# Rounding on ScalarE and two-deep loads in the weight quantisation of a transformer layer

## The chip, the cores and the metric

The program runs on all 8 cores of one Trainium2 chip, each with its own share of the batch and with a full copy of the weights to prepare. Time is device microseconds from the first to the last instruction of the slowest core; lower is better. The engines are TensorE (PE in the profile), VectorE (DVE), ScalarE (ACT), GpSimd (POOL) and SyncE (SP). SP and POOL also issue DMA transfers; each core has 16 DMA engines, shared by both queues.

## The reference

One layer, 16 sequences of 2048 x 1024 float32: attention with 16 heads, then a feed-forward block whose weights are quantised to -1, 0 and 1, each with layer norms and a residual.

```python
def weight_quant(w):
    scale = 1.0 / jnp.clip(jnp.mean(jnp.abs(w)), 1e-05)
    return jnp.clip(jnp.round(w * scale), -1, 1) / scale
def bit_linear(x, w):        # act_quant: 8 bits for each row of x
    return einsum('bsd,hd->bsh', act_quant(x), weight_quant(w))
x = x + layernorm(attn(layernorm(x)))
h = silu(depthwise_conv1d(bit_linear(layernorm(x), w1)))   # w1: 4096 x 1024
x = x + layernorm(bit_linear(h, w2))                       # w2: 1024 x 4096
```

## The kernel before

Each core takes two sequences and all weights. Its work is cut into stages by an all-engine barrier of the core: the setup (weights), then per sequence layer norm, the q, k and v products, attention, the output product, and last the two feed-forward products. No core waits for another.

The setup writes prepared weights to DRAM, from where later stages load them. It first casts wq, wk, wv and wo to bf16 (eight batches of 2 MB; stores of wqkv_sp at L235). Then `quant_weight` runs for w1 and after it for w2, each 16 MB in float32, in `nbatch` = 8 batches of 2 MB: a tile `stg[sl]` (named wstg in the profile) of 128 x 4096. For w1 one batch is one block of 128 rows of 16 KB, for w2 four blocks of 4 KB rows. There are two such tiles, sl = c % 2, two output tiles `wqx` (wqa, wqb), and a single `qh16` in float16.

`quant_weight` has two passes. The absmean pass loads all batches and sums absolute values on DVE (L264 the load, L269 the sum), followed by a short chain that puts the scale into `wsc` (L273 to L293). The quantising pass loads all batches again (L311), and DVE does three operations for each: L316 multiplies by the scale, adds 1536 and rounds to an integer by writing float16 (qh16); L320 subtracts 1536 and takes the maximum with -1; L323 takes the minimum with 1. Then the batch is stored as bf16, 1 MB (L326).

In this pass even batches are loaded by SP, odd ones by POOL, and all stores are issued by POOL. Each engine's instructions run in program order, and the load of batch c stands in iteration c: behind a wait for the clamp (L323) of batch c-2, and on POOL behind the store of batch c-1, which waits for the clamp of that batch. `Sem.wait(engine, value)` makes an engine wait; without a value it waits for all that was issued so far. After w2 SP waits for all transfers, and the barrier at L334 ends the setup. `posRM` is a 128 x 1 tile that holds 1536. ScalarE is not used in the setup.

Of the kernel before, what the change touches and what calls it, by code (L numbers as in the profile page):

```python
# [12 lines left out]
AF = mybir.ActivationFunctionType  # L13
AX = mybir.AxisListType
OP = mybir.AluOpType
# [7 lines left out]
RM = 1536.0  # L23
# [16 lines left out]
def build_nc(dbg=()):  # L40
# [3 lines left out]
    def _un(n):  # L44
        _nctr[0] += 1
        return f"{n}_{_nctr[0]}"
# [27 lines left out]
    V, S, TE, G, SY = nc.vector, nc.scalar, nc.tensor, nc.gpsimd, nc.sync  # L74
# [8 lines left out]
    with es:  # L83
# [14 lines left out]
        posRM = sbuf("posRM", [128, 1], F32)  # L98
        wsc = sbuf("wsc", [128, 4], F32)
# [21 lines left out]
        sv, ss, st, sg = (sems[k] for k in ["tv", "ts", "tt", "tg"])  # L121
        dxr = [sems["dxr0"], sems["dxr1"], sems["dxr2"], sems["dxr3"]]
        dstg = [sems["dst0"], sems["dst1"]]
        dss = [sems["dss0"], sems["dss1"]]
# [54 lines left out]
        qh16 = _ph.enter_context(nc.sbuf_tensor(_un("qh16"), [128, DH], F16))  # L179
# [3 lines left out]
        with _ph:  # L183
            stg = [wstg0, wstg1]
# [34 lines left out]
            for i, (wh, b) in enumerate([(w, k) for w in range(3) for k in range(2)]):  # L219
                eng = SY if i % 2 == 0 else G  # L220
                if i >= 2:
                    sv.wait(eng, castv[i - 2])
                lv = dstg[i % 2].inc(eng.dma_start(
                    stg[i % 2][:, 0:4 * H].rearrange("p (c n) -> p c n", n=H),
                    wsrc[wh][b * 512:(b + 1) * 512, :].rearrange(
                        "(c p) n -> p c n", p=128)), 16)
# [13 lines left out]
            for b in range(2):  # L240
                sl = b % 2
                eng = SY if sl == 0 else G
                sv.wait(eng, castv[-2])
                lv = dstg[sl].inc(eng.dma_start(
                    stg[sl][:, 0:4 * H].rearrange("p (c n) -> p c n", n=H),
                    wo_h[b * 512:(b + 1) * 512, :].rearrange(
                        "(c p) n -> p c n", p=128)), 16)
# [4 lines left out]
            def quant_weight(src_h, nchunk, width, sw_col, dst_sp, mwcol=None):  # L252
                nb = DH // width
                nbatch = nchunk // nb
                bw = nb * width
                redv = []
                sv.wait(SY)
                sv.wait(G)
                for c in range(nbatch):
                    if c >= 2:  # L260
                        sv.wait(SY, redv[c - 2])
                        sv.wait(G, redv[c - 2])
                    eng = SY if c % 2 == 0 else G
                    lv = dstg[c % 2].inc(eng.dma_start(  # L264
                        stg[c % 2][:, 0:bw].rearrange("p (c n) -> p c n", n=width),
                        src_h[c * nb * 128:(c + 1) * nb * 128, :].rearrange(
                            "(c p) n -> p c n", p=128)), 16)
                    dstg[c % 2].wait(V, lv)
                    redv.append(sv.inc(V.tensor_reduce(  # L269
                        nrm[:, c % 16:c % 16 + 1], stg[c % 2][:, 0:bw],  # L270
                        axis=AX.X, op=OP.add, apply_absolute_value=True)))
                sv.wait(V)
                sv.inc(V.tensor_reduce(nrm[:, 20:21], nrm[:, 0:nbatch],  # L273
                                       axis=AX.X, op=OP.add))
                sv.wait(TE)
                tq1 = st.inc(TE.matmul(pst[0:1, 0:128], nrm[:, 20:21], identf[:],  # L276
                                       start=True, stop=True))
                st.wait(V, tq1)
                sv.inc(V.tensor_reduce(nrm[0:1, 21:22], pst[0:1, 0:128],
                                       axis=AX.X, op=OP.add))  # L280
                sv.wait(TE)
                tq2 = st.inc(TE.matmul(pst[:, 0:1], ones1f[:], nrm[0:1, 21:22],
                                       start=True, stop=True))
                st.wait(V, tq2)
                sv.inc(V.tensor_copy(nrm[:, 21:22], pst[:, 0:1]))
                sv.wait(V)
                sv.inc(V.reciprocal(nrm[:, 22:23], nrm[:, 21:22]))
                sv.wait(V)
                nel = float(nchunk * 128 * width)
                sv.inc(V.tensor_scalar(wsc[:, sw_col:sw_col + 1], nrm[:, 22:23], nel,  # L290
                                       None, op0=OP.mult))
                if mwcol is not None:
                    sv.inc(V.tensor_scalar(wsc[:, mwcol:mwcol + 1], nrm[:, 21:22],  # L293
                                           1.0 / (nel * 127.0), None, op0=OP.mult))
                sv.wait(V)
                qv = [0, 0]
                qst = [0, 0]
                sv.wait(SY)
                sv.wait(G)
                dss[0].wait(V)  # L300
                dss[1].wait(V)
                dsq[0].wait(V)
                dsq[1].wait(V)
                for c in range(nbatch):
                    sl = c % 2
                    if c >= 2:
                        sv.wait(SY, qv[sl])
                        sv.wait(G, qv[sl])
                        dss[sl].wait(V, qst[sl])
                    eng = SY if c % 2 == 0 else G  # L310
                    lv = dstg[sl].inc(eng.dma_start(  # L311
                        stg[sl][:, 0:bw].rearrange("p (c n) -> p c n", n=width),
                        src_h[c * nb * 128:(c + 1) * nb * 128, :].rearrange(
                            "(c p) n -> p c n", p=128)), 16)
                    dstg[sl].wait(V, lv)
                    sv.inc(V.tensor_scalar(qh16[:, 0:bw], stg[sl][:, 0:bw],  # L316
                                           wsc[:, sw_col:sw_col + 1], RM,
                                           op0=OP.mult, op1=OP.add))
                    sv.wait(V)
                    sv.inc(V.tensor_scalar(wqx[sl][:, 0:bw], qh16[:, 0:bw],  # L320
                                           -RM, -1.0, op0=OP.add, op1=OP.max))
                    sv.wait(V)
                    qv[sl] = sv.inc(V.tensor_scalar(wqx[sl][:, 0:bw], wqx[sl][:, 0:bw],  # L323
                                                    1.0, None, op0=OP.min))
                    sv.wait(G, qv[sl])
                    qst[sl] = dss[sl].inc(G.dma_start(  # L326
                        dst_sp[c * nb:(c + 1) * nb].rearrange("c p n -> p c n"),
                        wqx[sl][:, 0:bw].rearrange("p (c n) -> p c n", n=width)), 16)

            quant_weight(w1t_h, KC, DH, 0, w1qt_sp, mwcol=1)  # L330
            quant_weight(w2t_h, HC, H, 2, w2qt_sp)
            for s_ in (dstg[0], dstg[1], dss[0], dss[1], dsq[0], dsq[1], dc):
                s_.wait(SY)
# [4 lines left out]
        with _ph:  # L338
            A3 = attA[:, :].rearrange("p (c n) -> p c n", n=T)

            for s in range(NSEQ):
# [7 lines left out]
                with _ph:  # L349
# [6 lines left out]
                    for i in range(NT128):  # L356
# [3 lines left out]
                        if i >= 2:  # L360
                            st.wait(S, lnuse[i % 2])
                        sev = ss.inc(S.activation(ln1b[i % 2][:], xr[i % 3][:], AF.Identity,  # L362
                                                  scale=r_ap, bias=mb_ap))
# [39 lines left out]
                with _ph:  # L403
# [36 lines left out]
                    for oc in range(OC):  # L440
# [5 lines left out]
                        if oc + 1 < OC:  # L446
                            sl2 = (oc + 1) % 2
                            eng = SY if sl2 == 0 else G
# [4 lines left out]
                        for j in range(NT512):  # L453
# [18 lines left out]
                            for kc in range(KC):  # L472
# [10 lines left out]
                                                      bias=bq_pre[:, oc:oc + 1]))  # L483
# [5 lines left out]
                                                      scale=1.0, bias=bv_pre[:, oc:oc + 1]))  # L489
# [95 lines left out]
                with _ph:  # L585
# [80 lines left out]
                    for g in range(NPAIR * NSTEP):  # L666
                        p, i = divmod(g, NSTEP)
                        qc, kt = divmod(i, NKT)
                        sl = g % 2
                        if pend[0] is not None and i in (2, 10, 18, 26):  # L670
                            flush_tailA((2, 10, 18, 26).index(i))
                        if i == 2 * NKT + 4 and pend[0] is not None:
# [7 lines left out]
                            bias=negM[:, p:p + 1], scale=1.0))  # L680
# [53 lines left out]
                with _ph:  # L734
# [11 lines left out]
                    for g in range(8):  # L746
# [34 lines left out]
                        for i in range(2):  # L781
# [7 lines left out]
                                                      scale=r3, bias=mb3))  # L789
# [17 lines left out]
                        for i in range(2):  # L807
# [8 lines left out]
                                                      scale=r2, bias=mb2))  # L816
# [8 lines left out]
                                                   None, op0=OP.max))  # L825
# [14 lines left out]
                                                   op0=OP.mult, op1=OP.add))  # L840
# [3 lines left out]
                                op0=OP.add))  # L844
# [59 lines left out]
        with _ph:  # L904
# [18 lines left out]
            for s in range(NSEQ):  # L923
# [81 lines left out]
                for ti in range(NT128):  # L1005
# [14 lines left out]
                                           op0=OP.max))  # L1020
# [4 lines left out]
                                           None, op0=OP.mult))  # L1025
# [40 lines left out]
        with _ph:  # L1066
# [79 lines left out]
            for idx in range(NSJ):  # L1146
# [6 lines left out]
                for i2 in range(2):  # L1153
                    for half in range(2):
# [4 lines left out]
                            for c in range(HC):  # L1159
                                base = c * 512 + (i2 * 2 + half) * 128  # L1160
                                for hh in range(2):
# [13 lines left out]
                                                      scale=r4, bias=mb4))  # L1175
# [49 lines left out]
```

How the kernel before makes its waits and increments, by code:

```python
    def inc(self, ins, n=1):  # L31
        ins.then_inc(self.h, n)
        self.v += n
        return self.v
# [1 line left out]
    def wait(self, eng, v=None):  # L36
        eng.wait_ge(self.h, self.v if v is None else v)
```

## Time and profile before

| | us |
|---|---|
| median of the runs shown (2 runs) | 4776.24 |
| lowest and highest of them | 4764.93, 4787.56 |
| the profiled execution | 4804.53 |
| its span, slowest core (core 0) | 4802.9 |
| spans of the other cores | 4744.0 to 4796.4 |

The profile shows one execution. Its page gives for each engine the busy share in 40 equal slices of the span (one slice is 120 us). In the timeline a line is one instruction: start, duration, engine, source line, operation, output and input tiles, and in brackets how long the engine had been idle and what ended that. SPq and POOL lines with DMA_DIRECT2D are the issue of a transfer, not the transfer itself. In the table of windows each line gives, for a stretch of time, the busy time of each engine with its number of instructions, then TensorE's granted clock (1.00 is full), the mean busy share of the 16 DMA engines and what they moved in GB/s.

### The profile page before, as it was taken

To read this page: it belongs to the slowest core of one execution; us is meant where nothing else is said; L and a number is where in the kernel's file an instruction comes from. 1 tells how busy PE (TensorE), PEld (TensorE's weight loads), DVE (VectorE), ACT (ScalarE), POOL (GpSimd) and SP (SyncE) were. 2 spreads that over 40 slices of the span, in tenths; PEclk is the share of its full clock that TensorE was granted. 3 is DMA by queue.
4 is the path that set the end of the run, shared out by engine and by line. 5 is a ranking of instruction groups with operands and counts; after the bars stand their busy time and mean duration, and the time that the engine had idled before them with its cause. 6 is when DMAs were issued, how large, how long until landed. Compare 5 with 4: busy or idle time off the path is not lost. (4 is left out here: it accounts for less than half of the span.)

```text
span 4802.9 us, 42027 instructions; the slowest of 8 cores (4744.0 to 4802.9 us)
## 1 busy us (share of the span) xinstructions
PE 2892.2 (60%) x12214; PEld 1071.8 (22%) x12366; DVE 2091.1 (44%) x3552; ACT 1786.7 (37%) x2139; POOL 67.6 (1%) x110
## 2 busy tenths in 40 slices
PE   0000177888884231687888852329985986476877
PEld 0000033222221111332222211113332332132333
DVE  1443434446464444343555554434443444334332
ACT  0000133878782212337787832112221221424231
POOL 0001000000000000000000000000000000000000
PEclk9999999999996665899999976559997997687888
DMA  7675200000000222100000002231111111432231
GB/s 202 239 233 196 95 33 20 1 5 3 5 3 22 68 77 75 42 20 1 5 3 5 3 13 70 70 131 40 49 49 53 49 46 49 147 123 70 97 114 66
DMA packets 152903, 311.67 MB, mean 65 GB/s; under 512 B 65445, under 2 KB 98277, under 8 KB 148582
## 3 DMA queue, kind: packets, MB, share of 16 engines
q1 hardware_dynamic: 134570, 218.76, 14.0%
q0 software_dynamic: 18112, 90.22, 5.5%
q8 instruction: 108, 1.77, 0.2%
q14 instruction: 113, 0.93, 0.1%
HBM read 206.16 MB, written 98.60 MB: 63 GB/s over the span
## 5 line engine op out<-in xcount | busy, mean ns | idle before, releaser
L678 ACT ACTIVATE ptil<-sc,negM 128x1024 bf16<-128x1024 f32 x1024 | 1043.1, 1147 | 208.3 <-PE sc L617 208.1
L691 PE MATMUL accB<-ptil,vres 128*65 128x512 bf16 x1024 | 398.0, 389 | 57.5 <-DVE tmpB L701 57.5
L614 PE MATMUL sc<-qres,kres 64*128 64x512 bf16 x1024 | 396.0, 387 | 51.9 <-ACT ptil L678 4.5
L687 PE MATMUL accA<-ptil,vres 128*65 128x512 bf16 x1024 | 425.6, 416 | 0.9 <-ACT ptil L678 0.8
L617 PE MATMUL sc<-qres,kres 64*128 64x512 bf16 x1024 | 407.5, 398 | 0.0
L1162 PE MATMUL p2a<-w2q,ring 128*128 128x512 bf16 x1004 | 258.1, 422 | 166.5 <-DVE outt L1179 139.5
L159 ACT ACTIVATE stat<-stat 128x1 f32<-128x1 f32 x128 | 26.0, 203 | 722.3 <-DVE stat L154 720.1
L988 ACT ACTIVATE hsb<-pcA,convb_s 128x512 bf16<-128x512 f32 x128 | 87.9, 687 | 537.1 <-PE pcA L979 481.4
L851 PE MATMUL pw<-ident,xqtm 128*128 128x128 bf16 x256 | 32.4, 306 | 417.7 <-DVE xqtm L842 417.7
L955 PE MATMUL pwA<-xqd,w1q 128*128 128x512 bf16 x1004 | 251.1, 392 | 42.7 <-DVE hsc L964 40.8
L699 DVE COPY lbufB<-accB 1x512 f32<-1x512 f32 x64 | 43.8, 685 | 484.7 <-PE accB L691 484.7
L955 PE MATMUL pwB<-xqd,w1q 128*128 128x512 bf16 x1004 | 247.5, 388 | 1.2
L159 ACT ACT_TABLE_LOAD x4 | 5.1, 1283 | 633.4 <-DVE stat L154 633.4
L1162 PE MATMUL p2b<-w2q,ring 128*128 128x512 bf16 x1002 | 236.7, 396 | 1.4
L276 PE MATMUL pst<-identf,nrm 128*1 128x128 f32 x4 | 1.2, 396 | 367.6 <-DVE nrm L273 367.6
L614 PEld LDWEIGHTS sc<-qres,kres 64*128 64x128 bf16 x1024 | 95.1, 93 | 526.7 <-issue 526.7
L627 DVE RECIPROCAL invrA<-lbufA 1x512 f32<-1x512 f32 x64 | 211.7, 3307 | 1.7
L629 DVE RECIPROCAL invrB<-lbufB 1x512 f32<-1x512 f32 x64 | 210.0, 3282 | 0.0
L373 PE MATMUL ptrA<-ident,ln1b 128*128 128x128 bf16 x128 | 18.7, 300 | 313.3 <-ACT ln1b L362 313.3
L640 PE MATMUL pib<-invrA,ones1f 1*64 1x512 f32 x128 | 101.2, 883 | 137.6 <-DVE invbB L650 79.3
L1162 PEld LDWEIGHTS p2a<-w2q,ring 128*128 128x128 bf16 x1024 | 107.4, 106 | 319.2 <-issue 259.3
L993 DVE TENSOR_TENSOR macc<-macc,hsb 128x2048 bf16<-128x2048 bf16 x64 | 78.4, 1225 | 217.3 <-ACT hsb L988 217.3
(203 smaller groups left out, 4335.9 us busy)
## 6 DMA issues: line engine op xcount, KB each, us to landing
hs_sp<-hsb SPq DMA_DIRECT2D x64, 512.0 KB, 2.7
ring<-hs_sp SPq DMA_DIRECT2D x8, 4096.0 KB, 15.0
wstg<-w1t SPq DMA_DIRECT2D x8, 2048.0 KB, 10.8
wstg<-w1t POOLq DMA_DIRECT2D x8, 2048.0 KB, 13.5
wstg<-w2t SPq DMA_DIRECT2D x8, 2048.0 KB, 11.0
wstg<-w2t POOLq DMA_DIRECT2D x8, 2048.0 KB, 15.5
xra<-x SPq DMA_DIRECT2D x32, 512.0 KB, 3.6
xrb<-x SPq DMA_DIRECT2D x32, 512.0 KB, 4.4
```

The source lines that it names most:

```text
L614: TE.matmul(sc[sl][:, 0:512], kc_[0:64, kt * 128:(kt + 1) * 128], qc_[0:64, qc * 512:(qc + 1) * 512], start=True, stop=True, tile_position ...
L617: smmv[g] = st.inc(TE.matmul(sc[sl][:, 512:1024], kc_[64:128, kt * 128:(kt + 1) * 128], qc_[64:128, qc * 512:(qc + 1) * 512], start=True, ...
L627: V.reciprocal(invrA[0:1, r * 512:(r + 1) * 512], lbufA[0:1, r * 512:(r + 1) * 512])
L629: erv_ = sv.inc(V.reciprocal(invrB[0:1, r * 512:(r + 1) * 512], lbufB[0:1, r * 512:(r + 1) * 512]))
L640: TE.matmul(pib[0:64, :], ones1f[0:1, 0:64], invrA[0:1, r * 512:(r + 1) * 512], start=True, stop=True, tile_position=(0, 0))
L678: expv[pl] = ss.inc(S.activation(ptil[pl][:], sc[sl][:], AF.Exp, bias=negM[:, p:p + 1], scale=1.0))
L687: TE.matmul(accAd[:], dc4[:, kt, 0:65], ptil[pl][:, 0:512], start=(kt == 0), stop=(kt == NKT - 1))
L691: avv3[pl] = st.inc(TE.matmul(accB[:], dc4[:, kt, 65:130], ptil[pl][:, 512:1024], start=(kt == 0), stop=(kt == NKT - 1)))
L955: _ins = TE.matmul(pwx[slw][:], w1q[:, kc * DH + c * 128:kc * DH + (c + 1) * 128], xqd[:, kc * T + j * 512:kc * T + (j + 1) * 512], start= ...
L988: silv[slc] = ss.inc(S.activation(hsb[:, j * 512:(j + 1) * 512], pcx[slc][:], AF.Silu, bias=convb_s[:, c:c + 1], scale=1.0))
L993: V.tensor_tensor(macc[:], macc[:], hsb[:], op=OP.max)
L1162: _ins = TE.matmul(pp[:, hh * 512:(hh + 1) * 512], ring[slr][:, base:base + 128], w2q[:, c * H + hh * 512:c * H + (hh + 1) * 512], start=( ...
```

## The change

The edit is in the quantising pass of `quant_weight` alone. Batches 0 and 1 are loaded ahead of the loop. In iteration c ScalarE does the multiply, the add of 1536 and the rounding into qh16 (an Identity activation with the scale `wsc` and the bias `posRM`, both read from 128 x 1 tiles); then the load of batch c+2 into the tile just read is placed (`qload`), still on SP for even and POOL for odd batches, behind waits for the rounding of batch c. The two operations of DVE on qh16 and wqx stay. Stores are issued by SP. ScalarE waits, before it rounds, for all DVE work issued so far, hence for the clamp of the batch before.

```diff
@@ -295,35 +295,50 @@
                 sv.wait(V)
                 qv = [0, 0]
                 qst = [0, 0]
+                roundv = [0, 0]
                 sv.wait(SY)
                 sv.wait(G)
                 dss[0].wait(V)
                 dss[1].wait(V)
                 dsq[0].wait(V)
                 dsq[1].wait(V)
+                lvs = {}
+
+                def qload(c_):
+                    sl_ = c_ % 2
+                    if c_ >= 2:
+                        sv.wait(SY, qv[sl_])
+                        sv.wait(G, qv[sl_])
+                        ss.wait(SY, roundv[sl_])
+                        ss.wait(G, roundv[sl_])
+                    eng_ = SY if c_ % 2 == 0 else G
+                    lvs[c_] = dstg[sl_].inc(eng_.dma_start(
+                        stg[sl_][:, 0:bw].rearrange("p (c n) -> p c n", n=width),
+                        src_h[c_ * nb * 128:(c_ + 1) * nb * 128, :].rearrange(
+                            "(c p) n -> p c n", p=128)), 16)
+
+                qload(0)
+                if nbatch > 1:
+                    qload(1)
                 for c in range(nbatch):
                     sl = c % 2
                     if c >= 2:
-                        sv.wait(SY, qv[sl])
-                        sv.wait(G, qv[sl])
                         dss[sl].wait(V, qst[sl])
-                    eng = SY if c % 2 == 0 else G
-                    lv = dstg[sl].inc(eng.dma_start(
-                        stg[sl][:, 0:bw].rearrange("p (c n) -> p c n", n=width),
-                        src_h[c * nb * 128:(c + 1) * nb * 128, :].rearrange(
-                            "(c p) n -> p c n", p=128)), 16)
-                    dstg[sl].wait(V, lv)
-                    sv.inc(V.tensor_scalar(qh16[:, 0:bw], stg[sl][:, 0:bw],
-                                           wsc[:, sw_col:sw_col + 1], RM,
-                                           op0=OP.mult, op1=OP.add))
-                    sv.wait(V)
+                    dstg[sl].wait(S, lvs[c])
+                    sv.wait(S)
+                    roundv[sl] = ss.inc(S.activation(
+                        qh16[:, 0:bw], stg[sl][:, 0:bw], AF.Identity,
+                        scale=wsc[:, sw_col:sw_col + 1], bias=posRM[:, 0:1]))
+                    if c + 2 < nbatch:
+                        qload(c + 2)
+                    ss.wait(V)
                     sv.inc(V.tensor_scalar(wqx[sl][:, 0:bw], qh16[:, 0:bw],
                                            -RM, -1.0, op0=OP.add, op1=OP.max))
                     sv.wait(V)
                     qv[sl] = sv.inc(V.tensor_scalar(wqx[sl][:, 0:bw], wqx[sl][:, 0:bw],
                                                     1.0, None, op0=OP.min))
-                    sv.wait(G, qv[sl])
-                    qst[sl] = dss[sl].inc(G.dma_start(
+                    sv.wait(SY, qv[sl])
+                    qst[sl] = dss[sl].inc(SY.dma_start(
                         dst_sp[c * nb:(c + 1) * nb].rearrange("c p n -> p c n"),
                         wqx[sl][:, 0:bw].rearrange("p (c n) -> p c n", n=width)), 16)
```

## Rows read from the trace of the kernel before

**Rows 1.** The page: its first line, and the busy tenths of 40 slices.

```profile
span 4802.9 us, 42027 instructions; the slowest of 8 cores (4744.0 to 4802.9 us)
...
PE   0000177888884231687888852329985986476877
...
DVE  1443434446464444343555554434443444334332
ACT  0000133878782212337787832112221221424231
...
DMA  7675200000000222100000002231111111432231
```

**Rows 2.** Timeline of the quantising loop of w1, core 0: start us, duration, instruction.

```profile
183.21 0.33 SPq L311 DMA_DIRECT2D wstg<-w1t  x1
191.42 2.35 DVE L316 TENSOR_SCALAR qh<-wstg,wsc 128x4096 f16<-128x4096 f32 x1 [8.29 <-DMA wstg<-w1t]
...
215.43 2.35 DVE L316 TENSOR_SCALAR qh<-wstg,wsc 128x4096 f16<-128x4096 f32 x1 [18.99 <-DMA wstg<-w1t]
217.89 1.23 DVE L320 TENSOR_SCALAR wqb<-qh 128x4096 bf16<-128x4096 f16 x1
...
225.46 0.33 SPq L311 DMA_DIRECT2D wstg<-w1t  x1
...
226.46 0.53 POOL L311 DMA_DIRECT2D wstg<-w1t  x1
244.84 2.35 DVE L316 TENSOR_SCALAR qh<-wstg,wsc 128x4096 f16<-128x4096 f32 x1 [19.47 <-DMA wstg<-w1t]
...
296.77 2.35 DVE L316 TENSOR_SCALAR qh<-wstg,wsc 128x4096 f16<-128x4096 f32 x1 [13.35 <-DMA wstg<-w1t]
...
300.57 1.23 DVE L323 TENSOR_SCALAR wqb<-wqb 128x4096 bf16<-128x4096 bf16 x1
301.88 0.38 SPq L264 DMA_DIRECT2D wstg<-w2t  x1
```

**Rows 3.** Timeline of the quantising loop of w2, its start and its end, core 0.

```profile
371.82 0.37 SPq L311 DMA_DIRECT2D wstg<-w2t  x1
...
493.73 0.75 POOL L326 DMA_DIRECT2D w2qt_sp<-wqb  x1 [18.21 <-DVE wqb L323]
```

**Rows 4.** Table of windows, core 0: from and to us, engines, clock, DMA share, GB/s.

```profile
226.00:244.00 18.00, 0.00 (x0) 0.00 (x0) 0.00 (x0) 0.00 (x0) 0.99 (x2) 1.00 0.84 291
256.00:272.00 16.00, 0.00 (x0) 0.00 (x0) 0.00 (x0) 0.00 (x0) 0.39 (x1) 1.00 0.93 326
...
344.00:358.00 14.00, 0.00 (x0) 0.00 (x0) 8.79 (x3) 0.00 (x0) 0.74 (x1) 1.00 0.89 303
...
302.00:372.00 70.00, 1.14 (x4) 0.61 (x4) 36.18 (x13) 0.00 (x0) 3.52 (x5) 1.00 0.77 255
```

**Rows 5.** DMA view, core 0, 183 to 302 us in 40 slices of 3 us.

```profile
GB/s 88 391 226 0 0 165 341 355 416 352 132 0 0 184 168 253 352 386 352 358 61 0 0 231 187 259 300 405 397 325 11 0 0 264 308 253 303 281 0 0
```

**Rows 6.** Timeline, start of the absmean pass of w2, core 0.

```profile
302.87 0.75 POOL L264 DMA_DIRECT2D wstg<-w2t  x1
316.68 4.42 DVE L269 TENSOR_REDUCE nrm<-wstg 128x1 f32<-128x4096 f32 x1 [14.88 <-DMA wstg<-w2t]
```

**Rows 7.** Groups of ScalarE instructions: count, busy us, mean ns, idle us before.

```profile
L678 ACT ACTIVATE ptil<-sc,negM 128x1024 bf16<-128x1024 f32 x1024 | 1043.1, 1147 | 208.3 <-PE sc L617 208.1
L1134 ACT ACTIVATE q216a<-m216a,posRM 128x512 f16<-128x512 f16 x128 | 92.2, 720 | 127.1 <-DVE m216a L1123 126.4 <-DVE ring L1138 0.5
...
L988 ACT ACTIVATE hsb<-pcA,convb_s 128x512 bf16<-128x512 f32 x128 | 87.9, 687 | 537.1 <-PE pcA L979 481.4 <-DVE hsc L964 32.7 <-PE pwB L955 16.4
...
L362 ACT ACTIVATE ln1b<-xra,stat 128x1024 bf16<-128x1024 f32 x32 | 39.7, 1239 | 17.3 <-DVE stat L163 17.3
...
L159 ACT ACT_TABLE_LOAD x4 | 5.1, 1283 | 633.4 <-DVE stat L154 633.4
```

**Rows 8.** Timeline, SP issues four stores of wqkv_sp in the cast stage.

```profile
29.43 12.73 SPq L235 DMA_DIRECT2D wqkv_sp<-wqb  x4
```

## The prediction

> **What bounds the kernel now.** I read the page first, for where in the span the edited code lies. In the slices of the span TensorE and ScalarE are idle through the first four slices of 120 us and DVE stands at one to four tenths, while the 16 DMA engines are at five to seven tenths; the slowest core's span is 4802.9 us [rows 1]. So the setup before the first attention stage is some 500 us long, and no compute engine fills it. It ends in a barrier, so each microsecond taken from it comes off the end one for one, unless a later stage changes.
>
> Next the timeline of the two quantising loops of `quant_weight`, the code that is edited. For w1 the first load is issued at 183.21 and its multiply-add begins at 191.42, 8.2 us later. From then on batches come in pairs: multiply-adds of the odd batches start at 215.43 and 244.84 (and once more), with the next even batch right behind, then nothing: 19 to 19.5 us of idle DVE before the next pair, ended by the DMA into wstg. The reader should look at SP and POOL there: loads of an even batch leave at 225.46 and the odd one, on POOL, at 226.46, both only when the clamp of the even batch is done. The POOL load stands in program order behind the store of the batch before, which waits for a clamp. The last batch starts at 296.77 and is done at 300.57 + 1.23 = 301.80. The loop lasts 301.8 - 183.2 = 118.6 us [rows 2]. The w2 loop has the same shape: first load 371.82, last store issued 493.73; 121.9 us [rows 3].
>
> Last the DMA view and the table of windows, for what the transfers can do. While DVE quantises, nothing moves: in the 3 us slices there are pairs of 0 GB/s at each pair of batches [rows 5]. With loads and stores both open it is 291 GB/s (226 to 244) and 326 GB/s (256 to 272). In the absmean pass of w2, which loads all the time, one window has 303 GB/s at a DMA share of 0.89; the whole pass with its start and end 255 [rows 4]. The loops are therefore bound by a chain, load pair, then quantise pair, in which transfer and arithmetic alternate. A period of 29.4 us carries two loads of 2.1 MB and two stores of 1.05 MB, 6.3 MB, or 214 GB/s.
>
> **The change part by part.**
>
> *Loads ahead.* Batches 0 and 1 leave together; batch c+2 leaves when batch c is rounded into qh16, and odd loads no longer stand behind a store. The wait is now for DMA alone, if the arithmetic is shorter than the transfers.
>
> *Multiply-add to ScalarE.* Of DVE's 2.35 + 1.23 + 1.23 us a batch (L316, L320, L323) the 2.35 go [rows 2]. No ScalarE instruction of 4096 columns is in the trace. The same kind with two pointer operands takes 1.24 us at 1024 columns, one at 512 columns 0.72 [rows 7]: the slope (1.24 - 0.72)/512 gives 1.24 + 3072 x 1.02 ns = 4.4 us, the upper end. Two forms that read PSUM, 1.147 us at 1024 and 0.687 at 512, have a slope of 0.90 ns and give 1.15 + 2.76 = 3.9, the lower end. I take 4.0, near the lower end, since that slope comes from the row with by far the most instructions. So it is slower than the 2.35 us it replaces. As qh16 is single, batch c+1 is rounded only when the clamp of c is through: the chain for one batch is 4.0 + 0.2 + 2.6 + 0.2 = 7.0 us. A batch's transfers (3.15 MB) take 10.3 us at 305 GB/s. The slower rounding is thus hidden behind the transfers, except for the first and last batch; without that cover it would cost 8 x 1.65 = 13 us a weight. The ScalarE has no other work here [rows 1].
> The Trainium skill, "ScalarE: Activation LUTs", Rules for kernel authors, says to put multiplies and adds on VectorE, not ScalarE; the rows agree on the duration, not that it must cost time here. By its formula for ACTIVATE (same page, What ACT_TABLE_LOAD costs) an estimate for 4096 columns is 3.8 us, which would leave the sum within half a microsecond.
> A table load may now stand before the first rounding: 1.28 us [rows 7], once, at most; I count 1.3 lost.
>
> *Stores to SP.* 16 stores of 1 MB move from POOL to SP, behind SP's loads. Queued behind a store's wait (for the clamp) on SP is only the load of batch c+2 or c+3, which waits for the rounding of a later batch anyway. So nil, as long as issuing is short. POOL keeps only the eight odd loads of both weights here.
>
> *The new w1 loop:*
> (a) loads 0 and 1 land together. A like pair in the absmean pass, issued at 301.88 and 302.87, had its first user at 316.68, 14.4 us after 302.3 [rows 2, 6] (with a store still open); the 4.2 MB at 326 GB/s plus 1.8 us of start give 14.7; the first of the two comes a bit before: 13.7 us.
> (b) round batch 0 (4.0), hand over (0.2), first data of load 2: a lone load took 8.2 us where 2.1 MB at 326 GB/s are 6.4, so 1.8. Together 6.0 us in which DMA is idle.
> (c) loads 2 to 7 (12.6 MB) and the six stores mixed among them (6.3 MB): 18.9 MB. At what rate? The windows bound it by 291 and 326; I take 305, near the sustained one: 62 us.
> (d) after load 7: 4.0 + 0.2 + 2.6 = 6.8 us.
> Sum 13.7 + 6.0 + 62 + 6.8 = 88.5, against 118.6: 30 us saved. For w2 121.9 - 88.5 = 33 us.
> (e) Given back: at the loop's end two stores are now open and not one, 1.05 MB more at 305 GB/s = 3.4 us, once before w2's DMA-bound absmean pass, once before the barrier: 7 us. Table load 1.3.
> Saved: 30 + 33 - 7 - 1 = 55 us. The profiled execution took 4804.5 us, so it would take 4749; the median shown is 4776.2, 28 below the profiled one, and the forecast for it is 4776 - 55 = 4721 us. With 326 GB/s (c) is 58 us and 63 are saved; with 255, the whole absmean pass with its gaps, it is 74 us and 31 are saved.
>
> **The rivals.**
>
> *Pairs persist.* Two loads in flight share the DMA engines and may keep landing together. Then DMA idles until batch c is rounded: a pair takes 6.0 + 6.3 MB/305 = 26.6 us (29.4 before), and the loop 13.7 + 3 x 26.6 + 13.8 for two batches in series = 107 us. Saved 12 + 15 - 7 = 20: 4756 us. For it: two loads in flight land within one batch's work today. Against: load c+3 leaves 7 us after load c+2, since the roundings are serial, so the pair is pulled apart.
>
> *The common memory gives less once no core pauses.* Today some cores pause while others load. For it: one window of core 0 at 326 has no equal in the absmean pass. At 255 GB/s the saving is 31: 4745 us. Against: in the absmean pass all cores load all the time and still have about 300.
>
> *Bursts can be sustained.* In 3 us slices core 0 reaches 352 to 416 GB/s [rows 5]. At 360 in (c) 52.5 us: 40 + 43 - 6 - 1 = 76 saved: 4700 us. Against: those are slices in which other cores may have been pausing.
> The Trainium skill, "DMA: Bandwidth & Descriptors", Bandwidth, gives about 358 GB/s for a core when both cores of a memory domain stream; the traced sustained 303 lies below it, the slices reach it. By that figure the sum would end at this rival's time.
>
> *Slower: SP's queue fills.* SP was held 12.73 us issuing the second four wqkv stores (1 MB in 256-byte pieces) [rows 8]. If each 1 MB store held SP that long, the even loads would be late: a pair would last 2 x 12.7 + 8.2 + 4.0 = 37.6 us, 8 more than now, four times a weight: about +66 us, 4842. It turns from gain to loss when a store holds SP for about 8.5 us. Against it: the new stores are cut into 8 KB (w1) or 2 KB (w2) rows, at most 512 pieces where those four had 4096, and a load in the 4 KB rows of w2 leaves SP in 0.37 us [rows 3].
>
> *It does nothing*: if loads and stores already filled the memory. Excluded by the 0 GB/s slices [rows 5].
>
> **How the numbers follow.** Forecast 0.52; memory gives less 0.15; pairs persist 0.13; bursts sustained 0.12; SP fills 0.02; something later in the kernel moves the total by more than 1% either way, such as the granted clock of the later stages, 0.06 (0.04 of it downwards, as the gain helps that side, 0.02 upwards). None of the first five leaves 4776 by 2% (95 us), which is about what a measurement of this kernel can tell from no change: to save 95 us both loops would have to fall to 71 us, in which (c) has 44 us, 430 GB/s, above every row. So within 2% 0.94, faster 0.04, slower 0.02. The range runs from bursts (4700) to pairs (4756); the two runs shown lie 11 us to either side of their median, which I add at the low end: 4690 to 4758.
>
> **What would show it.** After the change: the w1 loop (first load to last clamp) 85 to 92 us; ScalarE identity instructions of about 4.0 us, 16 of them; DVE's waits within the loop for ScalarE, ScalarE's for DMA; no 0 GB/s window longer than a few microseconds after batch 2; about 300 GB/s in the loop where a period had 214; the absmean pass of w2 some 3 us later to start moving; everything behind the barrier as before, some 55 us earlier. It would be wrong if loads still land in pairs with idle DMA between, if the loop's rate stays at 250 GB/s, if SP shows long issues, or if the later stages last otherwise than before.

## The result and the profile after

| | before | changed |
|---|---|---|
| median, us | 4785.31 | 4697.17 |
| all runs, us | 4764.93 to 4845.03 | 4692.19 to 4768.15 |
| ratio, with its 95% interval | | 0.983 (0.979 to 0.987) |

Some 81 us less (63 to 99), where 55 were forecast. Later the two kernels were run again, together on one chip, at 4784.9 and 4707.5 us, ratio 0.985 (0.983 to 0.987), 77 us less. A few runs in which one die's cores had a lower clock are left out of the ratios.

The page of the changed kernel, core 6 (first line, busy tenths of 40 slices):

```profile
span 4731.8 us, 42067 instructions; the slowest of 8 cores (4694.2 to 4731.8 us)
...
PE   0000487888883221787888853318885886376677
...
DVE  1333333464645444333555464443443444334333
ACT  0113234887871221337787842112221221423332
...
DMA  7776100000001222000000002240111110433231
```

ScalarE now has one tenth in the second and third slice, DVE is down to three tenths in the second and third where [rows 1] had four, and TensorE is busy for four tenths of the fifth slice where it had one: the stages behind the setup begin earlier.

The timeline of the w1 loop of the changed kernel, core 6 (start us, duration, engine, line; the rounding is L329, the maximum L335, the clamp L338, loads L315, stores L341). The first line joins two issues by SP, batch 0 at 186.61 and batch 2 at 204.87; the last joins the first loads of the pass behind the loop:

```profile
186.61 18.59 SPq L315 DMA_DIRECT2D wstg<-w1t  x2
187.09 0.53 POOL L315 DMA_DIRECT2D wstg<-w1t  x1 [16.35 <-DVE wsc L293]
199.69 1.28 ACT L329 ACT_TABLE_LOAD   x1 [199.69 <-DMA wstg<-w1t]
200.99 3.80 ACT L329 ACTIVATE qh<-wstg,posRM,wsc 128x4096 f16<-128x4096 f32 x1
...
211.91 0.90 POOL L315 DMA_DIRECT2D wstg<-w1t  x1 [24.29 <-ACT qh L329]
...
226.40 3.80 ACT L329 ACTIVATE qh<-wstg,posRM,wsc 128x4096 f16<-128x4096 f32 x1 [8.48 <-DMA wstg<-w1t]
...
235.08 3.80 ACT L329 ACTIVATE qh<-wstg,posRM,wsc 128x4096 f16<-128x4096 f32 x1 [4.88 <-DMA wstg<-w1t]
238.96 0.33 SPq L315 DMA_DIRECT2D wstg<-w1t  x1
242.93 1.23 DVE L335 TENSOR_SCALAR wqa<-qh 128x4096 bf16<-128x4096 f16 x1 [10.07 <-DMA w1qt_sp<-wqa]
...
245.90 3.80 ACT L329 ACTIVATE qh<-wstg,posRM,wsc 128x4096 f16<-128x4096 f32 x1 [7.02 <-DMA wstg<-w1t]
...
254.44 3.80 ACT L329 ACTIVATE qh<-wstg,posRM,wsc 128x4096 f16<-128x4096 f32 x1 [4.75 <-DMA wstg<-w1t]
...
263.19 0.32 SPq L341 DMA_DIRECT2D w1qt_sp<-wqa  x1
263.53 3.80 ACT L329 ACTIVATE qh<-wstg,posRM,wsc 128x4096 f16<-128x4096 f32 x1 [5.28 <-DMA wstg<-w1t]
...
268.77 1.23 DVE L338 TENSOR_SCALAR wqb<-wqb 128x4096 bf16<-128x4096 bf16 x1
...
270.48 35.19 SPq L264 DMA_DIRECT2D wstg<-w2t  x3
```

The reader should compare with [rows 2]. There the work of two batches stood side by side and then 19 us of nothing. Here the roundings of batches 3 to 7 start at 226.40, 235.08, 245.90, 254.44 and 263.53, some 9.3 us apart, and each waits for its own load: the loads no longer land in pairs. The loop lasts 270.0 - 186.6 = 83.4 us, where it was 118.6.

The table of windows for the same loop, columns as in [rows 4], and the DMA view of 186 to 270 us in 40 slices of 2.1 us, both of core 6:

```profile
186.60:199.70 13.10, 0.00 (x0) 0.00 (x0) 0.00 (x0) 0.01 (x1) 0.53 (x1) 1.00 0.84 288
199.70:206.00 6.30, 0.00 (x0) 0.00 (x0) 1.10 (x1) 5.08 (x2) 0.00 (x0) 1.00 0.23 78
206.00:218.00 12.00, 0.00 (x0) 0.00 (x0) 3.81 (x4) 7.60 (x2) 0.90 (x1) 1.00 1.01 336
218.00:236.00 18.00, 0.00 (x0) 0.00 (x0) 4.91 (x4) 4.72 (x2) 0.90 (x1) 1.00 0.97 311
236.00:254.00 18.00, 0.00 (x0) 0.00 (x0) 4.91 (x4) 6.68 (x2) 0.90 (x1) 1.00 1.01 333
254.00:270.00 16.00, 0.00 (x0) 0.00 (x0) 4.91 (x4) 7.60 (x2) 0.00 (x0) 1.00 0.69 264
```

```profile
GB/s 0 242 359 312 265 375 437 8 0 125 351 374 277 382 371 222 257 351 456 335 195 234 410 355 265 293 394 394 425 218 246 406 335 261 433 406 207 378 129 0
```

After one gap, from 201 to 205 us, the engines move 311 to 336 GB/s at a share near 1 until the last load has landed. The gaps of [rows 5] are gone.

### The profile page after: what moved, and what is told of

Its sections match the earlier page's. It is cut to its first block and busy times, and to the rows that moved or that the text cites. A ratio compares the mean times of both kernels' runs of the same rounds, so it can differ in the third digit from the quotient of the medians.

```text
span 4731.8 us, 42067 instructions; the slowest of 8 cores (4694.2 to 4731.8 us)
## 1 busy us (share of the span) xinstructions
PE 2882.1 (61%) x12214; PEld 1060.5 (22%) x12366; DVE 2054.1 (43%) x3536; ACT 1850.3 (39%) x2155; POOL 51.9 (1%) x94
## 5 line engine op out<-in xcount | busy, mean ns | idle before, releaser
L706 PE MATMUL accB<-ptil,vres 128*65 128x512 bf16 x1024 | 412.5, 403 | 58.9 <-DVE tmpB L716 58.9
L702 PE MATMUL accA<-ptil,vres 128*65 128x512 bf16 x1024 | 437.9, 428 | 1.0 <-ACT ptil L693 0.8
L629 PE MATMUL sc<-qres,kres 64*128 64x512 bf16 x1024 | 410.3, 401 | 39.6 <-ACT ptil L693 4.7
L632 PE MATMUL sc<-qres,kres 64*128 64x512 bf16 x1024 | 418.9, 409 | 0.0
L1177 PE MATMUL p2a<-w2q,ring 128*128 128x512 bf16 x1004 | 237.4, 397 | 180.9 <-DVE outt L1194 154.3
L159 ACT ACTIVATE stat<-stat 128x1 f32<-128x1 f32 x128 | 26.0, 203 | 708.5 <-DVE stat L154 708.5
L1177 PE MATMUL p2b<-w2q,ring 128*128 128x512 bf16 x1002 | 222.3, 379 | 1.2
L388 PE MATMUL ptrA<-ident,ln1b 128*128 128x128 bf16 x128 | 18.7, 300 | 270.9 <-ACT ln1b L377 270.9
L702 PEld LDWEIGHTS accA<-ptil,vres 128*65 128x65 bf16 x1024 | 112.5, 110 | 255.8 <-issue 255.8
## 6 DMA issues: line engine op xcount, KB each, us to landing
wstg<-w1t POOLq DMA_DIRECT2D x8, 2048.0 KB, 13.7
```

Source lines behind the costliest of these rows:

```text
L629: TE.matmul(sc[sl][:, 0:512], kc_[0:64, kt * 128:(kt + 1) * 128], qc_[0:64, qc * 512:(qc + 1) * 512], start=True, stop=True, tile_position ...
L632: smmv[g] = st.inc(TE.matmul(sc[sl][:, 512:1024], kc_[64:128, kt * 128:(kt + 1) * 128], qc_[64:128, qc * 512:(qc + 1) * 512], start=True, ...
L702: TE.matmul(accAd[:], dc4[:, kt, 0:65], ptil[pl][:, 0:512], start=(kt == 0), stop=(kt == NKT - 1))
L706: avv3[pl] = st.inc(TE.matmul(accB[:], dc4[:, kt, 65:130], ptil[pl][:, 512:1024], start=(kt == 0), stop=(kt == NKT - 1)))
L1177: _ins = TE.matmul(pp[:, hh * 512:(hh + 1) * 512], ring[slr][:, base:base + 128], w2q[:, c * H + hh * 512:c * H + (hh + 1) * 512], start=( ...
```

## The experiments

The experiments ran on three chips: e1 to e4 on one, e5 to e8 on a second, e11, e12 and the repeats of the two kernels on a third. The kernel before was timed beside each group, at 4784.9, 4781.8 and 4784.9 us, and each ratio is to the runs beside it. Stage times of e1 to e8 are compared with those of the repeats, so across chips. For each, the stages of the setup are read from the timelines of all eight cores: when the w1 scale is ready, the w1 loop (from there to the end of the last clamp), the absmean pass of w2, the w2 loop, from its last clamp to SP's first load of x behind the barrier, and the time of that load. The figures are means over the cores.

```
                    scale  w1 loop  absmean  w2 loop  drain  x load   median us   ratio (95%)
before, 1st profile 182.5   115.3    70.1    120.1    7.2    495.3    4785.3
changed, 1st        185.2    82.7    70.4     82.0    5.5    425.8    4697.2    0.983 (0.979-0.987)
before, again       190.0   118.5    71.1    121.1    7.2    508.0    4785.1    1.000 (0.997-1.002)
changed, again      189.0    83.7    70.8     83.1    5.5    432.2    4707.5    0.985 (0.983-0.987)
e1 loads ahead      189.0    85.5    69.6     82.6    7.2    433.8    4706.7    0.984 (0.981-0.986)
e2 ScalarE only     190.1   131.2    70.7    133.4    7.2    532.7    4813.8    1.006 (1.003-1.009)
e3 SP stores only   188.0    99.6    72.2     97.8    4.8    462.3    4738.8    0.991 (0.987-0.995)
e4 no ScalarE       188.9    81.0    72.0     82.9    4.8    429.6    4722.7    0.984 (0.980-0.987)
e5 POOL stores      189.2    81.9    70.6     82.3    7.6    431.5    4705.1    0.983 (0.981-0.986)
e6 resident         189.1    72.7    70.5     71.2    5.4    408.9    4682.1    0.978 (0.975-0.981)
e7 clamp twice      188.3    85.1    70.6     85.0    5.0    434.1    4718.4    0.985 (0.981-0.989)
e8 resident, DVE    187.3    71.5    69.2     69.9    5.1    402.9    4676.9    0.980 (0.974-0.985)
e11 round twice     190.4    96.9    70.1     96.3    5.4    459.1    4741.9    0.991 (0.989-0.993)
e12 stored twice    190.7   102.4    79.1     83.7    5.7    461.7    4737.0    0.991 (0.989-0.993)
```

**The theories.** A: the gain is the loads ahead, which let transfers and arithmetic overlap until bytes bind. B: it is the stores' move to SP, which frees the odd loads. C: it is the work taken from DVE.

### Each part alone

*e1, loads ahead only.* Of the changed kernel only `qload` and its calls stay:

```diff
-                    roundv[sl] = ss.inc(S.activation(qh16, stg[sl], AF.Identity, ...))
+                    roundv[sl] = sv.inc(V.tensor_scalar(qh16, stg[sl], wsc, RM, ...))
-                    qst[sl] = dss[sl].inc(SY.dma_start(
+                    qst[sl] = dss[sl].inc(G.dma_start(
```

> The changed kernel with only its loads ahead: the rounding is back on DVE, the stores back on POOL. Theory A (the gain is the loads ahead; ScalarE and the queue of the stores have no part): each quantising loop lasts 80 to 84 us (83.5 and 83 with the full change, 119 and 122 before), the setup ends at about 423 to 427 us (mean of the cores; 426 with the full change, 495 before), total within 5 us of the changed kernel. Theory B (the stores' move to SP is what frees the odd loads): loops near 107 us. Theory C (DVE relieved by ScalarE): loops of 90 us and more.

Loops of 85.5 and 82.6 us. From the scale to the first load of x it takes 244.8 us, where in the repeats the kernel before takes 318.0 and the changed one 243.2: this part alone brings 73 of the 75 us. By the medians it is 78 us on its chip, where the whole change brought 77 on the third. Theory A stands; the w1 loop is a microsecond or two above the expectation. Its timeline, core 3, one of the slower ones:

```profile
221.43 2.35 DVE L328 TENSOR_SCALAR qh<-wstg,wsc 128x4096 f16<-128x4096 f32 x1 [5.49 <-DMA w1qt_sp<-wqa]
...
236.24 2.35 DVE L328 TENSOR_SCALAR qh<-wstg,wsc 128x4096 f16<-128x4096 f32 x1 [9.80 <-DMA w1qt_sp<-wqb]
...
239.17 0.88 POOL L315 DMA_DIRECT2D wstg<-w1t  x1 [11.63 <-DVE qh L328]
```

The rounding stands on DVE behind DVE's wait for an earlier store, and the load behind the rounding. In the changed kernel that wait (10.07 us before the maximum at 242.93 above) holds DVE only; ScalarE had already rounded at 235.08 and the load had left at 238.96. But that is not what makes e1's w1 loop longer: in e4 below, too, the rounding stands behind such a wait (11.50 us at 237.15 on core 6), and its w1 loop is 81.0. In e1 the DMA share, from the issue of the third load to the landing of the last, was 0.83 to 0.87, where the changed kernel had 0.96 to 0.98. Why was not tried.

*e2, ScalarE only.* The kernel before, with L316 as an activation on ScalarE.

```diff
-                    dstg[sl].wait(V, lv)
-                    sv.inc(V.tensor_scalar(qh16, stg[sl], wsc, RM, ...))
-                    sv.wait(V)
+                    dstg[sl].wait(S, lv); sv.wait(S)
+                    ss.inc(S.activation(qh16, stg[sl], AF.Identity, scale=wsc, bias=posRM))
+                    ss.wait(V)
```

> The kernel before with only the rounding on ScalarE; order of loads and stores as before. Theory A: transfers and arithmetic still alternate, and each of 8 batches is 3.80 - 2.35 = 1.45 us longer, less nothing hidden: loops of about 119 + 12 = 130 us and 133 us, the setup ends at 518 us instead of 495, total +20 to +25 us. Theory C: loops shorter than before.

Loops of 131.2 and 133.4, +12.5 us a loop; in all +29 us by the medians, +25 by the first load of x, where 20 to 25 were expected. Where transfers and arithmetic alternate, a slower rounding is paid in full. Theory C falls. Core 1, where the pause is that of [rows 2]: of its 21.76 us ScalarE waits 2.76 for DVE's two operations and 19.0 for the load:

```profile
225.55 3.80 ACT L317 ACTIVATE qh<-wstg,posRM,wsc 128x4096 f16<-128x4096 f32 x1 [21.76 <-DMA wstg<-w1t]
...
232.11 3.80 ACT L317 ACTIVATE qh<-wstg,posRM,wsc 128x4096 f16<-128x4096 f32 x1 [2.76 <-DVE wqb L324]
```

*e3, SP stores only.* The kernel before, with the one store line changed.

```diff
-                    sv.wait(G, qv[sl])
-                    qst[sl] = dss[sl].inc(G.dma_start(
+                    sv.wait(SY, qv[sl])
+                    qst[sl] = dss[sl].inc(SY.dma_start(
```

> The kernel before with only the stores issued by SP. The first odd load no longer stands behind a store, so batches pair as 0 1, 2 3 and so on, but the even load now stands behind a store. Theory A by the order of the queues: four pairs, 13.7 + 9.8 for the first and 18 + 9.8 for each other: 107 us a loop instead of 119, the setup ends near 471 us, total -24. Theory B: most of the 70 us gained.

Loops of 99.6 and 97.8, and 46 us less in all: twice what was expected, but by the expected pattern. The slowest core, 6:

```profile
203.48 2.35 DVE L316 TENSOR_SCALAR qh<-wstg,wsc 128x4096 f16<-128x4096 f32 x1 [13.37 <-DMA wstg<-w1t]
...
213.51 0.33 SPq L326 DMA_DIRECT2D w1qt_sp<-wqb  x1
213.93 0.39 SPq L311 DMA_DIRECT2D wstg<-w1t  x1
213.98 0.53 POOL L311 DMA_DIRECT2D wstg<-w1t  x1 [22.79 <-DVE wqb L323]
230.02 2.35 DVE L316 TENSOR_SCALAR qh<-wstg,wsc 128x4096 f16<-128x4096 f32 x1 [16.60 <-DMA wstg<-w1t]
```

The even load now stands behind a store on SP, so both loads of a pair leave together, after both clamps. A pair takes 25.5 to 26.5 us on this core (27.8 expected), and there are four full pairs instead of one single batch, three pairs and one single batch: four waits for loads instead of five. Theory B is not empty: this part alone is worth 46 us. But it gives nothing more once the loads are ahead, as the next two show.

### Each part taken from the whole

*e4, all but ScalarE,* and *e5, stores back on POOL:* the changed kernel with the first, or the second, of the two edits shown for e1.

> The changed kernel with the rounding back on DVE; loads ahead and stores on SP stay. Theory A: the rounding is hidden except for the first and the last batch of a loop, where DVE is 1.45 us quicker each: loops 2 to 4 us shorter than the changed kernel's 83, setup end 419 to 424, total 0 to 8 us below the changed kernel. Theory C: slower than the changed kernel by 10 us or more.

> The changed kernel with the stores back on POOL, rounding on ScalarE. Theory A: no change beyond 2 us in either loop, since what matters is that loads do not wait for a clamp. Rival D (stores behind the loads in SP's queue cost DVE the waits for a store to land that stand in the trace of the changed kernel, 8 to 10 us each for the even batches): loops 3 to 6 us shorter.

With DVE rounding (e4) the stretch from the scale to the first load of x is 240.7 us, against 243.2; the ratios are 0.984 and 0.985. e4's median of 4722.7 is no sign of a slower setup: the first load of x came at 429.6, against 432.2. With the stores on POOL (e5) it is 242.3; the loops are 1 to 2 us shorter, and the drain behind the last clamp is 2 us longer. Rival D, that SP's queue costs 3 to 6 us a loop, does not show. So with loads ahead neither edit is worth anything that can be measured here.

### What binds the loop now

*e7, the clamp done twice,* *e11, the rounding done twice* (the second on ScalarE, of the same operands), and *e12, each w1 batch stored twice,* the second time to the area of w2:

```diff
+                    sv.wait(V)                            # e7
+                    qv[sl] = sv.inc(V.tensor_scalar(wqx[sl], wqx[sl], 1.0, None, op0=OP.min))
...
+                    ss.wait(S)                            # e11
+                    roundv[sl] = ss.inc(S.activation(qh16, stg[sl], AF.Identity, ...))
...
+                    if src_h is w1t_h:                    # e12
+                        qst[sl] = dss[sl].inc(SY.dma_start(w2qt_sp[c * 4:(c + 1) * 4], wqx[sl]))
```

> The changed kernel with the clamp to 1 done twice: 1.33 us more in the chain of every batch (6.6 to 7.9 us; the transfers of a batch take about 9.5). Theory A (bytes bind): a loop is longer only by the last batch and the first one or two, 1.3 to 4 us, setup end +3 to +8. Rival E (the chain rounding, maximum, minimum binds): +10.6 us a loop, setup end +21.

> The changed kernel with the rounding on ScalarE done twice for each batch: the chain of a batch grows from 6.6 to 10.4 us, past the 9.1 us in which its 3.15 MB move at 340 GB/s. Theory A (the cover is the transfers of a batch): a loop becomes 13 + 8 x 10.4 = 97 us, +14 us each, setup end +28; of the 30 us a loop of added work half is still hidden. Rival E (the chain bound already): +30 us a loop.

> The changed kernel with each batch of w1 stored a second time, to a DRAM area that the w2 loop fills later: 4.2 instead of 3.15 MB a batch, w1 loop only. Theory A (all bytes count alike in the rate that binds): about six more stores before the last load lands, 6.3 MB at 328 GB/s: the w1 loop is 19 to 22 us longer. Rival F (loads bind, stores move beside them): +0 to +6 us. The w2 loop stays.

e7: 1.33 us more work a batch, 10.6 a loop, of which 1.4 and 1.9 us are seen against the changed kernel. The chain of 7.9 us a batch is hidden. e11: 30 us more work a loop, of which 13.2 are seen, near the 14 expected. Its timeline, core 7, shows the chain bare; behind the first batch each rounding waits for the clamp, no longer for a load:

```profile
218.97 3.80 ACT L329 ACTIVATE qh<-wstg,posRM,wsc 128x4096 f16<-128x4096 f32 x1 [2.76 <-DVE wqa L342]
222.86 3.80 ACT L333 ACTIVATE qh<-wstg,posRM,wsc 128x4096 f16<-128x4096 f32 x1
...
229.42 3.80 ACT L329 ACTIVATE qh<-wstg,posRM,wsc 128x4096 f16<-128x4096 f32 x1 [2.76 <-DVE wqb L342]
...
239.88 3.80 ACT L329 ACTIVATE qh<-wstg,posRM,wsc 128x4096 f16<-128x4096 f32 x1 [2.76 <-DVE wqa L342]
```

It is 10.45 us a batch. So the cover runs out between a chain of 7.9 and one of 10.4 us, where the 9.3 us between two landed loads lie.

e12: the w1 loop is 18.7 us longer, the w2 loop unchanged (83.7), as theory A had it; rival F, that only loads bind, falls. The stretch in which bytes bind, from the first data of the third load to the landing of the last, on core 6 of the changed kernel (repeat) and of e12, columns as in [rows 4]:

```profile
210.90:269.30 58.40, 0.00 (x0) 0.00 (x0) 15.97 (x14) 22.80 (x6) 2.69 (x3) 1.00 0.98 322
```

```profile
206.70:277.90 71.20, 0.00 (x0) 0.00 (x0) 13.54 (x12) 22.80 (x6) 1.95 (x3) 1.00 1.01 323
```

Over the eight cores it is 58.7 us for 18.9 MB in the changed kernel and 71.7 us for 23.1 MB in e12, 322 GB/s in both: 4.2 MB of stores more, at the same rate. The other 6 us of the 18.7 come at the end of the loop, 12.5 us instead of 6.6, since the maximum of batch 6 then waits for a store (15.74 us on core 6). Stores and loads count alike in one rate. Whether the DMA engines or the memory set that rate was not tried. Besides, the absmean pass behind it grew from 70.8 to 79.1 us: stores left open at the end of a loop are paid for there, but only here.

### Fewer bytes

*e6, resident.* The last two batches of the absmean pass still lie in the staging tiles when the scale is ready; they are quantised first, without a load. *e8* is the same with the rounding on DVE.

```diff
+                order = [nbatch - 2, nbatch - 1] + list(range(nbatch - 2))
...
-                qload(0)
-                if nbatch > 1:
-                    qload(1)
+                lvs[0] = dstg[0].v
+                lvs[1] = dstg[1].v
```

> The changed kernel, quantising the last two batches of the absmean pass first: they are still in the staging tiles, so two of eight loads of each loop and the wait for the first are gone. Theory A (the loop is bound by its bytes after a start of 13 us): a loop saves the 13 us start and keeps (c): about 6.5 + 62 = 70 us, setup end near 400, total -26 us against the changed kernel. Rival: the arithmetic of the first two batches is not hidden by anything and the loop is 75 us.

> Both loops with the last two batches taken from the staging tiles and the rounding on DVE, loads ahead, stores on SP. Theory A: the start of a loop is arithmetic alone, so DVE's quicker rounding shows in the first, second and last batch: 3 to 5 us a loop less than with the rounding on ScalarE; setup end near 392, total -30 to -35 us against the changed kernel.

e6 saves 11.0 and 11.9 us a loop against the changed kernel, and the first load of x comes 23 us earlier (26 expected); against the kernel before, each on its own chip, e6 is 100 us quicker and the changed kernel 77. e8 takes off another 1.2 us a loop, less than the 3 to 5 expected, and its median is 5 us lower, its ratio (0.980) no better than e6's; the intervals overlap, so e8's difference from e6 stays open. e6 beats both kernels, at 0.978 (0.975 to 0.981) of the kernel before. Its start, core 7; compare with the wait of 13 us above:

```profile
194.99 0.14 DVE L293 TENSOR_SCALAR wsc<-nrm 128x1 f32<-128x1 f32 x1
195.22 1.28 ACT L331 ACT_TABLE_LOAD   x1 [195.22 <-DVE wsc L293]
196.51 3.80 ACT L331 ACTIVATE qh<-wstg,posRM,wsc 128x4096 f16<-128x4096 f32 x1
200.39 0.33 SPq L318 DMA_DIRECT2D wstg<-w1t  x1
```

### Was anything changed behind the setup?

> The kernel before, unchanged, profiled on the same chip as the changed one. The change saved 72 us of setup in the two profiles (mean of the cores, from the first use of the w1 scale to the first load of x), while the medians lie 88 us apart. Theory A: nothing behind the setup changed; the stages behind it last 4255 to 4265 us (mean of the cores) in every kernel, and before's 4279 in its first profile went with that execution's lower granted clock. Rival: the stages behind the setup are 10 to 15 us longer in the kernel before, here too.

> The changed kernel, unchanged, on the same chip. Theory A: setup end 70 to 74 us earlier than in the kernel before on this chip, stages behind it within 5 us of those of the kernel before, ratio 0.983 to 0.986.

In the first pair of profiles the first load of x comes 69.5 us earlier while the medians lie 88 apart. Medians of the cores, from the profiles of the repeats, the kernel before first:

```profile
die 0 (median of its cores): 4768.7 us, clock 0.865
die 1 (median of its cores): 4773.2 us, clock 0.865
```

```profile
die 0 (median of its cores): 4694.3 us, clock 0.862
die 1 (median of its cores): 4695.5 us, clock 0.862
```

The mean span over the cores is 4769.9 us before and 4693.5 after. Less the first load of x (508.0 and 432.2) it is 4261.9 and 4261.3 us for all stages behind the setup; in e1 to e12 it is 4255 to 4265, but for e4 with 4273, where cores 4 to 7 had a clock of 0.85. So nothing measurable changed there, and the 76 us between the spans are the setup's. In the first pair of profiles the stretch from the scale to the first load of x is 312.8 and 240.6 us, 72 apart, which lies inside the interval of 63 to 99 us measured there; what of the other 9 us is chance was not settled. The stages behind the setup go with the granted clock there (before: 4296 us on cores 0 to 3 at 0.852, 4262 on cores 4 to 7 at 0.865), so these two profiles can't settle it.

## Why the prediction was right, and by how much it was off

The time (4697) lies in the range (4690 to 4758), near its low end, and within 2% as forecast (0.983, with an interval that reaches 0.979; 0.985, 0.983 to 0.987, in the repeat). The mechanism was right: transfers and arithmetic alternated, and do so no more. The saving was put at 55 us and is 76 to 81.

That the time lies in the range is in part luck. Its low end came from the rival of sustained bursts (4700), whose 360 GB/s were not reached, and 4697 lies inside by the 11 us of scatter added to it; the sum itself, at its higher rate of 326 GB/s, gave 63 us and 4713. The w1 loop was to last 85 to 92 us and lasts 81.0 to 84.0 on the eight cores in the first profile. And one sign was not as told: DVE does not wait for ScalarE alone, but before the maximum of some even batches for an earlier store (10.07 us at 242.93 above), which delays no rounding here.

Term by term, the windows from core 6 and the means over the cores from the repeat:

- *Which part does it.* The prediction costed the rounding on ScalarE as hidden and the stores' move as nil, so the gain was the loads ahead. e1, e4 and e5 bear that out. Not foreseen was that the stores' move alone is worth 46 us (e3), since it lets load 1 leave with load 0 and so takes one of five waits out of a loop.
- *The rounding.* 3.80 us where 4.0 was taken between 3.9 and 4.4. The slope of 1.02 ns, the upper end, mixed two kinds: L362 reads scale and bias from tiles, L1134 the bias alone. From L362 (1.239 us at 1024 columns) to the new row of the same kind it is (3.80 - 1.24)/3072 = 0.83 ns. The time is just below the lower end, and at the 3.8 of the Trainium skill's formula ("ScalarE: Activation LUTs", What ACT_TABLE_LOAD costs), which this measurement confirms. The same page's rule to put such work on VectorE is borne out by e2 (+29 us) where nothing hides the rounding; where transfers hide it, following the rule gains nothing that shows (e4).
- *(a) and (b), the start.* 13.7 and 6.0 forecast, 13.1 and 6.3 in the windows, with the table load of 1.28 us inside the 6.3. Over the cores load 2 was to be issued 17.9 us after load 0 (19.7 less the 1.8 to its first data) and is at 16.9 in w1 and 14.9 in w2: 4 us in both. Two loads that leave together do not land together: load 0 after 11.6 and 10.9 us, load 1 after 14.5 and 13.9.
- *(c), the bytes.* 62 us at 305 GB/s forecast; 57.3 us at 327 on core 6. Over the cores, from the issue of load 2 to the last landing, 63.8 forecast, 59.9 and 61.4 measured (322 and 317 GB/s): 6 us in both. This is the first term that was mis-sized. The rate was taken near the 303 of the absmean pass, where the DMA share was 0.89; that pass also waits, for a load leaves only when the sum over an earlier batch is done. The window with a share of 0.93 and 326 GB/s [rows 4] was the better guide.
- *(d), the end.* 6.8 forecast, 6.6 measured.
- *(e), given back.* 7 us forecast, none found. The step said that two stores are open at a loop's end. But the second last store (issued at 263.19 on core 6) had the 6.6 us of the last batch's arithmetic to land, and did so 0.3 to 3.9 us before the last clamp on every core; so one store is open, as before. The absmean pass took 70.8 us against 71.1. The drain before the barrier even fell from 7.2 to 5.5 us. e12, with two stores a batch, shows that the effect exists (8 us) when more is queued. This is the second mis-sized term, 9 us.
- *The table load.* 1.3 us forecast as lost. It stands at 199.69, before the first rounding, so it is in the w1 loop as measured; in exchange the one that stood at L159 after the barrier is gone (three there now, four in [rows 7]).

The start, the bytes and the end make some 10 us in the two loops. Together 55 + 10 + 9 + 1 = 75 us, and from the scale to the first load of x 75 were measured. (A slip that moved nothing: to save 95 us both loops would have to fall to 69 us, not 71.)

The rivals: *pairs persist* falls, the roundings are 9.3 us apart. *The memory gives less once no core pauses* falls: with all cores loading almost without a pause the mean over the cores is 322 and 317 GB/s in the two loops, above the 305 of the sum. *Bursts sustained* comes nearest in time (4700), but for another reason: its rate of 360 was not reached, and the shorter start and the nothing given back did the rest. The 358 GB/s of the Trainium skill ("DMA: Bandwidth & Descriptors", Bandwidth) were not reached either, with the DMA engines at a share of 0.97 to 1.01. *SP's queue fills* falls: a store is issued in 0.32 or 0.33 us.

## What to carry to other kernels

Where a loop alternates between transfers and arithmetic, look in the code for what each load stands behind, in its own engine's program order: a load behind a store that waits for a result waits with it. Once loads are issued as soon as their tile is read, moving work between engines or stores between queues is worth at most 2 us a loop here, until the chain of one batch exceeds the time of its bytes (here between 7.9 and 10.4 us against 9.3). Then count bytes: data that a first pass left on the chip should be used first.

## What the runs showed of the hardware that was not expected

- Loads and stores count alike: 322 GB/s a core, mean of the eight at work, with 12.6 MB loaded and 6.3 stored, and 322 with 12.6 loaded and 10.5 stored (w1 loops of the repeat and of e12).
- In the w1 loop of e8 the two cores of each pair (0 and 1, 2 and 3, 4 and 5, 6 and 7) differ: 67.0 to 68.0 us on one at 332 to 344 GB/s, 73.8 to 75.9 on the other at 290 to 300, and in e1 80.8 to 83.6 against 87.5 to 88.9. The quick one is each time the core whose loop began first. In the changed kernel the pairs differ by less than 3 us. The cause was not tried.
- Behind the last clamp the drain to SP's first load of x takes 7.2 to 7.6 us in every kernel that stores from POOL (before, e1, e2, e5) and 4.8 to 5.7 in every kernel that stores from SP. Of the 1.7 us between the kernel before and the changed one, 0.4 lie before the landing of the last store (5.5 and 5.1 us behind the clamp), the rest after it. The cause was not tried.
